# A wait between the scatters of a group on Pool, in a graph network and mixture-of-experts kernel

## What is computed

```python
x = x + gnn0(layernorm(x), adj)          # graph attention
x = x + ffn0(layernorm(x))               # 8 experts, top 2
x = x + gnn1(layernorm(x), adj)          # GRU over the graph, below
x = x + ffn1(layernorm(x))               # 16 experts, top 2

def gnn1(h, adj):
    A = (adj != 0)
    for i in range(3):
        m = einsum('bnd,de->bne', h, weight[i])
        aggr = einsum('bst,bsd->btd', A, m)
        h = gru_cell(aggr, h, w_ih, w_hh, b_ih, b_hh)
    return h

def ffn1(x):
    probs = softmax(x @ gate_w + gate_b)
    top_probs, top_idx = top_k(probs, 2)      # then normalised over the two
    return sum over the 2 chosen experts e of
        top_prob * ((silu(x @ w1[e]) * (x @ w2[e])) @ w3[e])
```

## Time and profile before

| | |
|---|---|
| median of 3 runs | 1330.41 us (1330.07 to 1338.6) |
| profiled execution, its own time | 1332.74 us |
| its span, first to last instruction | 1331.0 us |
| busy: PE, weight load, DVE, ACT, Pool | 76%, 61%, 61%, 43%, 47% |
| scatters of the GRU stage | 128, 129.0 us of Pool |
| DMA, mean over the span | 74 GB/s |
| mean granted clock of TensorE | 0.857 of full speed |

### The profile page before, as it was taken

One profiled execution on the slowest core, in us unless ns is written; L12 is line 12 of the kernel. 1 busy time (PEld: TensorE's weight loads), 2 busy tenths in 40 slices (PEclk: granted clock), 3 DMA queues, 4 the chain that ended last, 5 costly groups with the idle time before them and its releaser, 6 DMA issues. The chain is left out here.

```text
span 1331.0 us, 28510 instructions
## 1 busy us (share of the span) xinstructions
PE 1012.3 (76%) x6752; PEld 816.7 (61%) x6753; DVE 805.5 (61%) x3187; ACT 566.6 (43%) x1436; POOL 629.5 (47%) x686
## 2 busy tenths in 40 slices
PE   3655665459999999299987979879861799999930
PEld 2544544359999999245544545545431799888830
DVE  5777677536566666347776867768652444444427
ACT  3555545224343433146544645546431333333325
POOL 3567767725555555301334253352545266666540
PEclk8766666579999999699989989889975799999975
DMA  4222331222222221122202032040003222222229
GB/s 117 67 74 82 86 97 38 63 71 70 69 69 71 69 69 54 60 64 64 77 20 88 8 95 81 14 128 8 30 27 81 74 82 79 83 79 81 70 85 323
DMA packets 126206, 98.74 MB, mean 74 GB/s; under 512 B 33864, under 2 KB 115400, under 8 KB 126152
## 3 DMA queue, kind: packets, MB, share of 16 engines
q1 hardware_dynamic: 105536, 61.24, 16.9%
q0 software_dynamic: 17152, 35.29, 8.1%
q10 hardware_dynamic: 3464, 1.59, 0.5%
HBM read 55.44 MB, written 42.62 MB: 74 GB/s over the span
## 5 line engine op out<-in xcount | busy, mean ns | idle before, releaser
L1435 POOL DMA_INDIRECT result<-e_y,e_ids x280 | 281.8, 1007 | 247.6 <-PE e_ps_h L1464 103.4
L1464 PE MATMUL e_ps_h<-e_xT,e_up_of 128*128 128x128 f32 x2240 | 281.5, 279 | 14.4 <-DVE e_hT L1558 9.2
L1464 PEld LDWEIGHTS e_ps_h<-e_xT,e_up_of 128*128 128x128 f32 x2240 | 266.9, 195 | 20.4 <-issue 16.0
L1479 PE MATMUL e_ps_y<-w_sb,e_hT 128*128 x1664 | 209.5, 276 | 0.7 <-ACT e_y L1516 0.6
L1479 PEld LDWEIGHTS e_ps_y<-w_sb,e_hT 128*128 128x128 f32 x1664 | 197.5, 192 | 1.2 <-issue 1.2
L375 POOL DMA_INDIRECT queue<-g_q_rows,g_q_slots x128 | 129.0, 1008 | 77.8 <-DVE g_q_gap L320 38.1
L375 POOL DMA_INDIRECT queue<-a_r_rows,a_r_slots x128 | 128.2, 1001 | 66.4 <-issue 43.8
L1532 DVE COPY e_up_of<-w_sb 128x512 f32 x280 | 114.7, 449 | 3.4 <-issue 0.9
L1558 DVE TENSOR_TENSOR e_hT<-e_ps_h,e_gate 128x512 f32<-128x512 f32 x72 | 49.4, 686 | 111.3 <-ACT e_gate L1512 108.4
L1503 ACT ACTIVATE e_hT<-e_ps_h,b_sb 128x128 f32<-128x128 f32 x272 | 77.6, 368 | 87.4 <-PE e_ps_h L1464 78.9
L1490 ACT ACTIVATE e_xT<-e_ps_x 128x256 f32<-128x256 f32 x140 | 56.4, 403 | 110.7 <-PE e_ps_x L1452 103.5
(11 more groups left out here) (218 smaller groups left out, 1894.1 us busy)
## 6 DMA issues: line engine op xcount, KB each, us to landing
e_xq<-queue SPq DMA_DIRECT2D x280, 64.5 KB
g_y<-result SPq DMA_DIRECT2D x16, 512.0 KB
o_y<-result SPq DMA_DIRECT2D x16, 512.0 KB, 5.3
w_sb<-w SPq DMA_DIRECT2D x48, 128.0 KB
result<-e_y,e_ids POOLq DMA_INDIRECT x280
x_res<-x SPq DMA_DIRECT2D x16, 256.0 KB
w_sb<-w SPq DMA_DIRECT2D x16, 256.0 KB
out<-x_res SPq DMA_DIRECT2D x16, 256.0 KB, 4.6
```

The source lines that it names most:

```text
L1435: pool.indirect_dma_start(out=result, out_offset=bass.IndirectOffsetOnAxis(ap=ids[at_down.k][:, t, :].bitcast(U32), axis=0), in_=y[at_down ...
L1464: last = pe.matmul(ps_h[b][:, t, q * P:(q + 1) * P], up_of[at_up.k % 4][:, t, q * P:(q + 1) * P], xT[at_up.k % 4][:, t, :], start=True, st ...
L1479: last = pe.matmul(ps_y[b][:, t * D:(t + 1) * D], hT[at_down.k % 4][:, t, q * P:(q + 1) * P], down[:, bass.ds(e * (chunks * P) + q * P, P) ...
```

## The change

`queue_rows` gets a flag `apart`. Where it is set, Pool waits ahead of each scatter m of the group but m = 0, until `r.queued` has reached the count of the group's m scatters ahead of it, and a nop that carries the wait keeps it ahead of the DMA. The flag is set for the late group's two halves, and for group (n-1, 0) in steps that have a run.

```diff
-def queue_rows(pool, c, r, V, A, queue, at, first=0, last=TOPK * G):
+def queue_rows(pool, c, r, V, A, queue, at, first=0, last=TOPK * G, apart=False):
 
     wait(pool, V, "slots", at.s)
     wait(pool, A, "rows_copied", at.s)
     alone(pool, c)
-    for k, t in [divmod(m, G) for m in range(first, last)]:
+    for m in range(first, last):
+        k, t = divmod(m, G)
+        if apart and m:
+            pool.wait_ge(r.queued[at.b], 16 * TOPK * G * at.half + 16 * m)
+            alone(pool, c)
         pool.indirect_dma_start(
...
                 if late:
-                    queue_rows(pool, c, r, VK, AT1, c.queue1, late, 0, 4)
+                    queue_rows(pool, c, r, VK, AT1, c.queue1, late, 0, 4, True)
                 if has_tail:
                     rstd_and_shift(pool, c, tail_norm, VT, GT, AT0, group(n - 1, 0))
                 if late:
-                    queue_rows(pool, c, r, VK, AT1, c.queue1, late, 4)
+                    queue_rows(pool, c, r, VK, AT1, c.queue1, late, 4, apart=True)
...
                 if has_tail:
-                    queue_rows(pool, c, r, VK, AT1, c.queue1, group(n - 1, 0))
+                    queue_rows(pool, c, r, VK, AT1, c.queue1, group(n - 1, 0), apart=has_run)
                 if has_tail and not has_run:
                     queue_rows(pool, c, r, VK, AT1, c.queue1, group(n - 1, 1))
```

## The result

| | before | after |
|---|---|---|
| median | 1330.24 us (1326.81 to 1338.6, 4 runs) | 1498.77 us (1493.67 to 1503.22, 4 runs) |
| profiled execution, its own time | 1332.74 us | 1498.63 us |
| span | 1331.0 us | 1496.9 us |
| mean granted clock of TensorE | 0.857 | 0.819 |
| busy: PE, DVE, ACT, Pool | 76%, 61%, 43%, 47% | 69%, 54%, 38%, 42% |

The ratio is 1.1255, with a 95% interval of 1.1192 to 1.1318: 168.5 us slower, where +136 was forecast. It lies inside the range, nearer its slow end.

The account below looks back on a forecast made before the run. In the GRU stage ACT stands behind Pool, and Pool would stand behind scatter landings: S1 +113.7, S2 +22.3, S3 0, sum +136.0 us on 1332.74, less 2.3 for the median, 1466 us; range 1425 to 1530 us.

Parts of the forecast that it names:

- the one on the slack: Twelve scatters ahead of the first `g_tail_rstd`: Pool has 5.17 us of slack; beyond it each microsecond on Pool costs ACT one.
- the pause: At the loop's turn ACT, DVE and PE pause 7.68, 9.04 and 7.79 us; it stays, hidden under S1, adding nothing.
- S1: First scatter to first `g_tail_rstd`, seven stretches: 34.8 us each, 243.3 in sum against 129.59, so +113.7 us.
- Cadence: Time between scatter starts on Pool: from 1.26 us to landing 2.30 plus release 0.89, 3.19, taken as 3.25 us.
- The bounds 2.6 and 4.5: Limits in us on the cadence: packets just moved and a faster release below, the 3.74 us landing as the rule above.
- The loads' term: Three scatters in each of five S1 beside SP's loads may land a microsecond later; 0.06 us added to the mean cadence.
- S2: First to second `g_tail_rstd`, seven stretches: four cadences, 13.0 us each against 68.66 in sum before, so +22.3 us.
- S3: Second `g_tail_rstd` to next first scatter, six stretches, 146.87 us: unchanged as PE is busy throughout; 15 us at most from PE's clock.
- the rival at 0.03: Scatters lengthen the loop's pause by delaying something that comes by DMA; spaced, the pause shrinks: -22 us, 1308 us, chance 0.03.
- A landing disturbed everywhere: Rival: the 3.74 us landing is the rule, cadence 3.9 us and up, 1530 to 1589 us; chance 0.12.
- one under 2 us: Rival: landing quicker than the wake-up rows say, cadence 2.6 us, 1405 us; chance 0.08 including what lies up to 1425.
- waits already met: Rival of no change: counts are reached when Pool comes to the new waits; within 1%, chance 0.03.

Follow-up runs that it names:

- e3: The changed kernel with the new waits in group (n-1, 0) alone, none in the late group: 1403.75 us, 1.0566 of the kernel before.
- e7: The changed kernel with SP's loads of the experts' results and weights moved early, into S3 of the step before: 1427.08 us, 1.1327 of the kernel before.
- e1: The changed kernel with each of the 98 new waits on slots long written, so already met: 1326.67 us, 1.001 of the kernel before.
- e8: The kernel before, no new waits, with SP's loads of the experts' results and weights moved early, into S3 of the step before: 1317.94 us, ratio 0.9944.

## Why the prediction was right, and where not

**What bounds.** Right: ACT stands behind Pool, and Pool behind the landings. ACT's 219.7 us for `g_tail_shift`, and a stage of 503 us on two chips whose other stages differ, show it. The step that failed is the one on the slack. I took it as 5.17 us, which is what the trace had, but it came of the pause; with e3's pause gone, or on the third chip, it is nil (`g_tail_rstd` has no idle time ahead of it). It did no harm to the sum, since S1 was worked out from Pool's own chain.

**Cadence.** The quiet value was read right: 3.15 and 3.19 us in the mean of the two S1 without loads, against 3.19 worked out from a landing of 2.30 and 0.89 from release to start. The bounds 2.6 and 4.5 hold it with room.

**The loads' term was mis-sized.** I took three scatters a step, each a microsecond later. Measured: two of a step, each 1.7 to 2.9 us later than the quiet ones, and e7 prices all of it at 20 us where I had 6 (98 x 0.06). Less the 0.89, 4.76 to 5.95 us are a landing of 3.9 to 5.1 us. None of my rows had timed a scatter beside loads. The 3.74 us, which I took for a disturbed landing, isn't one: from 682 to 687 us the DMA engines carry only scatters and one instruction packet, and nearly all of the scatters' packets have moved by 684.0; why DVE went on only at 686.07 is open. No landing that DVE waits for in after is over 2.48 us. So the upper bound of 4.5 us rested on a misread row.

**S1.** Forecast 34.8 each; measured 33.7 and 34.1 in steps without loads, 38.6 in the mean of the five with them (193.2 / 5). Sum 261.0 against 243.3. At 3.19 us, without loads, the forecast is 7 x 34.2 = 239.1 us, and e7 has 240.7; the loads add 20 to that, where the forecast had 4.2 of its 6 us in S1.

**S2.** Forecast 13.0, measured 12.4; +18.4 against +22.3. The term's form was right: four landings between the two `g_tail_rstd`.

**S3.** I took none of it, bound 15 us; it was +7.9. The reason I gave, that PE is busy for all of it, no longer holds. In before PE is idle 2.7 us of the six S3, in after 18.4 us. Windows of after, the first 6 us of S3 in step 3:

```profile
786.96:790.00 3.04, 1.29 (x10) 0.95 (x8) 1.58 (x4) 1.53 (x4) 1.25 (x2) 1.00 0.07 22
790.00:793.00 3.00, 2.79 (x10) 1.64 (x11) 2.93 (x8) 1.86 (x4) 0.00 (x0) 0.71 0.00 0
```

PE works 1.29 of the first 3.04 us. I had also passed over a wait: DVE needs the landing of the late group's last scatter for `tail_ids`, and is idle 6.90 us until 788.38, 1.4 us into S3: that group is of a step before, as I wrote, but its scatters are issued in this step. PE's granted clock over all of S3 is 0.93 and 0.87 in the two rows shown, where it was 1.00; it is lower some way into it and not at its start. But S3 is 155 us also in the third chip's kernel before, at 0.96 to 1.00, with work that a short S2 leaves to it. How much of the 7.9 is the clock, and how much the idle time, is not told apart.

**The pause.** Wrong: I said that it stays and is hidden. It is gone, and what the rival at 0.03 said, that the scatters lengthen it, is what e1 and e3 show on their chip. Its reason, that the turn needs something by DMA, is not shown, and the turn is not needed. Its outcome, a faster kernel, still did not come, for the reason given there: it decides only while Pool is not later than ACT, a cadence under 1.8 us. ACT's wait of 27.80 us instead of 15 is the check on this: without the pause ACT comes to its wait 12.63 us into the stretch where it was 21.48, 8.85 us earlier, and the wait ends 18.21 us later, and 0.74 + 8.85 + 18.21 = 27.80. The wait at the second `g_tail_rstd`, forecast at about 5 us, was 5.28.

**The other rivals.** A landing disturbed everywhere, or one under 2 us, or waits already met: none. The fit that the prediction cites from the Trainium skill (DMA: Bandwidth & Descriptors, Anatomy of one DMA — SWDGE (gpsimd) path) gave a cadence of 3.04 us: the shortest of the quiet ones are 3.03, and their mean is nearer mine. Its 1445 us would have been 54 us low.

**Other stages.** 8 us in the result lie outside the three stretches; on the third chip it is -4 us (1444.54 - 502.66 against 1260.77 - 315.06), so they are no steady effect of the change.

## To carry over

A wait for a DMA's landing on the engine that issues it turns a stream of one start each 1.26 us into one each 3.1 to 3.2 here, and 4.8 to 5.95 where SP's large loads run beside; multiply it by the number of waits between two points at which another engine needs this one. Measure the slack that a trace shows for where it comes from: here it was a pause of others, and it left together with it. And before a stretch is called free of a pause, look at every instruction in it and not at one. Putting what others wait for ahead of what only has to be done, with more buffers to pay for it, was worth 20 us here.

## What the runs showed that I had not expected

- The same kernel takes 1330 us in the result and on the first chip, and 1259 to 1261 on two others. Of these 70 us 30 lie in the GRU stage's three stretches (345.1 against 315.1), where the pause is what the two traces show to differ; the rest lies outside them and was not looked into.
- On the first chip DVE's idle time at `x_res` is 7.6 us with scatters issued 1.3 us apart ahead of it (e1) and an ordinary wait of 1.4 us with two (e3). With SP's large loads out of the way (e8) it is 4.0 us, and a second standstill of 4 to 5.5 us follows.
- ACT stands still, 5.97 us, also behind the loop's last step, where no turn is taken and SP loads nothing.
- One scatter of 64.5 KB beside SP's loads (260 to 340 GB/s from 738 to 744 us of after) lands some 4 to 5 us after its start, an estimate from the time between starts less 0.89 us. Alone it lands in 2.2 to 2.3 us by the same sum, and DVE goes on 2.30 to 2.48 us after its start.
